# Building one-hot tiles with one two-input instruction for four numbers, in a single-core attention kernel

## The reference

```python
q, k, v = (split_heads(x @ W + b) for W, b in ...)      # 2 batches, 16 heads, 4096 tokens, width 16
scores = einsum('bhqd,bhkd->bhqk', q, k) * scale
sparsity = scores.max(axis=-1) - scores.mean(axis=-1)
_, top_idx = top_k(sparsity, U)                          # U = 307 of 4096 queries for each head
attn = softmax(einsum(q[top_idx], k) * scale)
out = zeros_like(q).at[top_idx].set(attn @ v)
x = layernorm(x + out @ Wo + bo)
x = layernorm(x + rwkv_channel_mix(x))                   # sigmoid(xr Wr) * (relu(xk Wk)^2 Wv)
```

## Time and profile before

| what | value |
|---|---|
| median of the runs | 3358.51 us (3 runs, 3357.48 to 3361.5) |
| profiled execution | 3360.67 us, its span 3358.7 us |
| PE busy | 3050.7 us, 91% of the span |
| DVE busy | 2933.8 us, 87% |
| ACT busy | 2807.1 us, 84% |
| POOL busy | 1573.7 us, 47% |
| mean granted TensorE clock | 0.972 |

### The profile page before, as it was taken

One profiled execution on the slowest core, in us unless ns is written; L12 is line 12 of the kernel. 1 busy time (PEld: TensorE's weight loads), 2 busy tenths in 40 slices (PEclk: granted clock), 3 DMA queues, 4 the chain that ended last, 5 costly groups with the idle time before them and its releaser, 6 DMA issues.

```text
span 3358.7 us, 60170 instructions
## 1 busy us (share of the span) xinstructions
PE 3050.7 (91%) x16612; PEld 1447.7 (43%) x16612; DVE 2933.8 (87%) x5964; ACT 2807.1 (84%) x6118; POOL 1573.7 (47%) x2744
## 2 busy tenths in 40 slices
PE   6999899989989999998998999899998998997587
PEld 3343333444434434443443555444444433444376
DVE  4999999988989888898998999899999898896488
ACT  5999889988988998898898887799987898893455
POOL 3223022224534543653364664766555653556644
PEclk8999999999999999999999999999999999997799
DMA  6342333432241131023112252112251121112122
GB/s 183 83 121 82 85 83 86 78 12 35 39 34 27 33 40 33 15 39 34 33 33 43 48 51 45 35 35 38 41 46 33 38 40 15 33 21 12 18 83 69
DMA packets 263682, 163.72 MB, mean 49 GB/s; under 512 B 168946, under 2 KB 242866, under 8 KB 259250
## 3 DMA queue, kind: packets, MB, share of 16 engines
q1 hardware_dynamic: 255250, 156.41, 25.2%
q0 software_dynamic: 6144, 1.37, 0.5%
q10 hardware_dynamic: 1952, 2.10, 0.2%
HBM read 111.86 MB, written 47.86 MB: 48 GB/s over the span
## 4 chain that ended last, share of the span: by engine, by line
DVE 34%; PE 27%; ACT 21%; issue 14%; POOL 2%; DMA 1%; ACTq 0%; DVEq 0%; SPq 0%; POOLq 0%
DVE JK L1170 27%; ACT AB L1022 18%; PE DP L756 7%; PE CP L737 4%; PE CP L746 4%; ACT E L1057 1%; DVE SPr L1170 1%; PE BP L774 1%; PE PV L864 1%; DVE VF L1382 1%; PE PV L865 1%; DVE fst L1341 1%; PE BP L849 1%; PE PV L887 1%; PE BP L828 1%
## 5 line engine op out<-in xcount | busy, mean ns | idle before, releaser
L1170 DVE CUSTOM_DVE_ANT_0 JK<-DP,AB 128x1024 bf16<-128x1024 f32 x2048 | 2468.1, 1223 | 286.0 <-ACT AB L1022 103.4
L1022 ACT ACTIVATE AB<-CP 128x512 f32<-128x512 f32 x4096 | 2292.8, 623 | 271.9 <-PE CP L737 203.1
L756 PE MATMUL DP<-KS,QS 128*128 128x512 f16 x4096 | 1234.8, 383 | 49.7 <-DVE SPr L1170 41.6
L1603 POOL TENSOR_TENSOR SCR<-E 128x307 f16<-128x307 f32 x966 | 671.7, 707 | 562.0 <-ACT E L1057 555.8
L737 PE MATMUL CP<-KS,QS 128*128 128x512 f16 x2048 | 794.2, 388 | 52.6 <-ACT AB L1022 28.8
L746 PE MATMUL CP<-KS,QS 128*128 128x512 f16 x2048 | 792.9, 387 | 30.3
L756 PEld LDWEIGHTS DP<-KS,QS 128*128 128x128 f16 x4096 | 360.8, 99 | 350.9 <-DVE SPr L1170 145.9
L1057 ACT ACTIVATE E<-BP 128x307 f32<-128x307 f32 x913 | 435.6, 477 | 42.4 <-PE BP L849 37.5
L737 PEld LDWEIGHTS CP<-KS,QS 128*128 128x128 f16 x2048 | 197.7, 97 | 512.8 <-ACT AB L1022 422.0
L746 PEld LDWEIGHTS CP<-KS,QS 128*128 128x128 f16 x2048 | 197.2, 96 | 389.0 <-ACT AB L1022 345.1
L849 PE MATMUL BP<-QT,KA 128*128 128x307 f16 x913 | 270.9, 297 | 28.8 <-ACT QT L1049 19.6
(11 more groups left out here) (386 smaller groups left out, 3138.0 us busy)
## 6 DMA issues: line engine op xcount, KB each, us to landing
KS<-KTC SPq DMA_DIRECT2D x256, 128.0 KB
QS<-QSC SPq DMA_DIRECT2D x512, 64.0 KB
KA<-KTC SPq DMA_DIRECT2D x128, 128.0 KB
QN<-SCR SPq DMA_DIRECT2D x16, 544.0 KB, 3.4
SCR<-in_L_attn_x SPq DMA_DIRECT2D x16, 512.0 KB, 5.5
AO<-E SPq DMA_DIRECT2D x16, 512.0 KB, 7.0
VF<-in_L_attn_x SPq DMA_DIRECT2D x64, 128.0 KB, 2.2
VF<-AO SPq DMA_DIRECT2D x64, 128.0 KB, 2.2
```

The source lines that it names most:

```text
L756: r = pe.matmul(o[:, 512 * j:512 * j + 512], qs, ks[j][:, 0, :], start=True, stop=True)
L1022: act.activation(AB[p % 3][:, 512 * j:512 * j + 512], BANK["C%d" % j], ACT.Abs).then_inc(ab_full, 1)
L1170: dve.tensor_tensor_reduce(out=JK[p % 2][:], in0=BANK["D%d" % u], in1=AB[p % 3][:], scale=1.0, scalar=0.0, op0=ALU.add, op1=ALU.max, accum ...
L1603: pool.tensor_tensor(EL[a % NE], E[a % NE][:], EH[a % NE], ALU.subtract).then_inc(el_g, 1)
```

## The change

The 36 one-input comparisons of a group, each against a constant, become nine two-input comparisons. Each takes the same `fb` or `fa` four times over and compares it with four numbers from a new tile `numbers` (0 to 19, made once by POOL), each read again for all 160 or 96 columns. In the groups selected during the score steps, `ob` and `oa` used to be handed out two planes a step, over 8 + 10 steps; now four a step, over 4 + 5. In the tail it was four a step before too. A semaphore is raised by four at once, so POOL's four multiplications are released together. And `prelude(0)` waits for the end of `values(1)` before it clears its buffers, where before it cleared first.

```diff
         yield [("slots", g)]
...
-        m = 2 if gaps else 4
+        m = 4
         for j in range(0, 16, m):
             yield [("ob", g, j, m)]
         for j in range(0, A_COLS, m):
...
+        while state["arranged"] < HEAD0[g] or "v1" not in done:
+            yield []
         yield [("ka", 0), ("qgzero",)] if g == 0 else []
-        while state["arranged"] < HEAD0[g]:
-            yield []
...
+        numbers = sb("numbers", [128, A_COLS], F16)
...
+            def one_hot(o, v, j0, m, w):
+                return dve.tensor_tensor(o[:, j0:j0 + m, 0:w], v[:, 0:w].unsqueeze(1).broadcast_to([128, m, w]),
+                                         numbers[:, j0:j0 + m].unsqueeze(2).broadcast_to([128, m, w]), ALU.is_equal)
+
             def ob(g, j0, m):
...
-                for j in range(j0, j0 + m):
-                    dve.tensor_scalar(OB[:, j, 0:NT * n], fb[:, 0:NT * n], float(j), None, ALU.is_equal).then_inc(sel_ob, 1)
+                one_hot(OB, fb, j0, m, NT * n).then_inc(sel_ob, m)
 
             def oa(g, j0, m):
-                n = GROUPS[g][2]
-                for j in range(j0, j0 + m):
-                    dve.tensor_scalar(OA[:, j, 0:NT * n], fa[:, 0:NT * n], float(j), None, ALU.is_equal).then_inc(sel_oa, 1)
+                one_hot(OA, fa, j0, m, NT * GROUPS[g][2]).then_inc(sel_oa, m)
...
+                pool.iota(numbers[:], pattern=[[1, A_COLS]], base=0, channel_multiplier=0,
                           allow_small_or_imprecise_dtypes=True)
```

More of the change, by code:

```diff
@@ L1448, in setup @@
                 pool.iota(tokc[:], pattern=[[128, NT]], base=-L // 2, channel_multiplier=1,
+                          allow_small_or_imprecise_dtypes=True)
+                pool.iota(numbers[:], pattern=[[1, A_COLS]], base=0, channel_multiplier=0,
                           allow_small_or_imprecise_dtypes=True)
```

## The result

The changed kernel takes 3365.36 us (median of 20 runs, 3359.01 to 3369.65), the kernel before 3357.80 (20 runs, 3348.31 to 3363.91): a ratio of 1.0022, with a 95% interval of 1.0015 to 1.0029. That is 7.6 us slower; forecast was 17. The profiled execution took 3367.77 us, its span is 3365.8, 7.1 more than before. Of these 7.1, the first `JK` starts 4.0 later, the seven heads with comparisons take 9.2 more, the other heads 2.3 less, and the stretch behind the last `JK` 3.9 less. The last `JK` starts 11.0 us later than before, where 15 to 25 were forecast.

The account below looks back on a forecast made before the run. DVE bounds `ob` and `oa` steps (1.37 us against PE's 1.30), PE the rest. Seven groups +19.6, moved attention +1.4, tail -4: +17.0 us, forecast 3375.5 us (3368 to 3384, chance 0.45; wider range 3357 to 3392).

Parts of the forecast that it names:

- The price of the instruction: New DVE comparison at the slow rate, 1.04 ns a column: 0.74 us paid for a wide one, 0.47 for a narrow.
- pair-rate rival: New comparison runs at 0.53 ns a column: 3358.5 us, or 3349 with short waits too; chance 0.12.
- the waits: DVE's waits for POOL in comparison steps; group 1: 2.5 us removed in eight `ob` steps, 2.6 added in four rounds.
- My middle value: Group 1, three later `ob` rounds and first `oa` round: DVE waits 0.65 us each for POOL's backlog.
- The rival that DVE slips in at once: Waits of only 0.1 or 0.15 us a round, -9.8 us in all, 3366 us; chance 0.20.
- lost cover: Freed steps shorten only as far as PE allows: +1.4 us in group 1, +0.5 each in groups 4 and 5.
- the case I had named last: Prediction is wrong if `feed(0)`'s chain through POOL stretches by more than a wait beside each `ob` round.
- +4.2 was forecast: Group 1, wide and beside attention: net cost over 18 score steps from its first `ob`, +4.2 us.
- 2.1 us credited: Group 2's earlier wait of 3.4 us behind six POOL subtractions will hardly recur; 2.1 us of it credited.
- +0.7 forecast: Group 2's net cost over its 18 score steps, after the credit for its long wait: +0.7 us.
- Attention earlier and the tail: `prelude` nine steps sooner: +1.4 us in score steps, -4 in the tail, with 0 and -7 as its ends.

Follow-up runs that it names:

- The pair read: Changed kernel with every number stored twice and both inputs read as pairs of neighbours, same nine instructions and order: 3350.41 us, 0.9962 of the kernel before.
- The kernel with 252 at the new pace: Changed kernel with the earlier one-input comparisons, 36 a group, four planes a step, no tile numbers: 3372.50 us, 1.0029 of the kernel before.
- that with 18 two-number instructions a group: Two-input comparison with two numbers in one instruction, in the 18 steps and order of the kernel before: 3375.08 us, 1.0029 of it.
- the kernel with steps given back: Changed kernel with nine empty steps after `oa`, so attention starts when it did before: 3374.40 us, 1.0031 of the kernel before.
- the shifted kernel: Changed kernel with group 2's one-hots 14 steps later, behind the indirect DMAs of head 14: 3363.01 us, 0.9996 of the kernel before.
- both profiles: The changed kernel's first profile and that of its unaltered second run, which took 3369.20 us, 1.0017 of the kernel before.

## Why the prediction was half right

**The price of the instruction: right.** 0.817 and 0.549 us measured, 0.82 and 0.554 forecast, and an undisturbed round costs 1.88 and 1.61 us from maximum to maximum, 0.74 and 0.47 above 1.14. The pair read isolates the cause: with the numbers in pairs the same columns take 0.482 and 0.348 us, which is 0.52 ns for each column more, against 1.05. The Trainium skill ("Vector Engine (DVE) Microarchitecture Reference", section 5.1) has one element read 16 times as an input of a two-source operation on 2-byte operands run at one element a cycle, and a row read again and again at two; these runs agree in the factor of two, with 160 and 96 repeats. The pair-rate rival was wrong for the kernel as changed. As a mechanism its price was good: it gave 3358.5 us with the long waits and 3349 with the short ones, and the kernel with pairs had short waits (7.3 us with the tail's) and a ratio that makes 3345 us of 3357.8.

**The step that failed: the waits.** "I take 0.65 in the three later `ob` rounds and the first `oa` round", and "in eight `ob` steps the wait of 0.31". In the seven groups these terms came to 12.8 us of waits removed and 13.2 added, as good as nothing. Measured: 25.6 before, 9.4 after, so 16.2 us less.

Two things were wrong. Nearly half of the waits of before stood beside `oa`, where I had put none: in group 1 2.37 us there and 2.21 beside `ob`. And the new instruction doesn't come back into a backlog. It gets in behind the POOL instruction under way, and POOL pays. So a wait is had per exposed instruction, and there are 63 of them now, not 252. The kernel with 252 at the new pace had 31.7 us of waits, that with 18 two-number instructions a group 20.1, the changed one 9.4. My middle value lay between 0.31 and 1.25, and 0.2 was under both, though I had named "nothing" as a least too. The rival that DVE slips in at once, at 0.1 to 0.15 a round and 3366 us, had the mechanism right here. That its time was only 0.6 off is luck: its waits came to 9.4 us less and not 16.2, and what it lacked there is about what it lacked in the losses below.

**Part of it came back elsewhere.** With 13.5 us for the instructions and -16.1 for the waits the kernel with steps given back should gain 2.6 in its seven heads, and it loses 9.2. The rest is 11.8, where 5.7 of lost cover were forecast. In that kernel PE idles 9.9 us behind POOL in 30 steps each of heads 22 and 27, where before it did not; that is the case I had named last, "if `feed(0)`'s chain through POOL stretches". Whole heads blur this, since their clock differs between executions (head 22 has 4.4 of the 9.9 and lost 0.2). The 18 steps from the first `ob`, which the forecast was made for, are clearer. There the kernel with steps given back loses 10.6 us, and what the instructions and the waits don't explain is 3.6 and 5.9 us in groups 4 and 5, beside 4.4 and 5.5 of this idle time, and 3.7 in the other five groups together, where 4.7 of lost cover were forecast. In group 1 the 18 steps take 29.9 us against 29.8, where +4.2 was forecast.

What makes POOL late for PE is shown in part. The same pace and order with one-input comparisons have none of this idle time, and neither has the changed kernel once the multiplications are moved away from `ob`. So it takes both, the multiplications beside `ob` and the merged instruction. That the instruction does it only by holding POOL up is not shown: with pairs it is shorter, and the idle time is 11.2 us and not 9.7.

**Group 2: the reading of the earlier trace rows failed.** I took it that a backlog may shut DVE out, and that it would hardly happen again (2.1 us credited). It happened again and longer, 5.1 us, so head 14 gained nothing (0.0 and -0.4; +0.7 forecast, which is near by luck, since its other waits went). A backlog alone was not the cause, as the shifted kernel shows: there POOL is as busy, and DVE gets in. What stood ahead of the backlog was.

**Attention earlier and the tail: the sum about right, the parts not.** Forecast were +1.4 and -4. The stretch behind the last `JK` is 317.9 us against 321.8, so -3.9. But from the last instruction of `slots` to the first product pass 10.8 us (10.5 forecast, 13.5 before), which is -2.7; the part ahead of it is 5.1 us longer and not 1 shorter, and what follows `idx` 6.3 shorter. In the score steps heads 28 and 29 take 5.7 us less than before, also in the one-input kernel at the new pace, and 0.6 less with the steps given back: moved attention is a gain there and no loss. By the runs, giving the steps back costs 3 to 5 us (1.0031 against 1.0022 and 1.0017), with intervals that overlap. The first `JK`'s 4.0 us, in no part of the forecast, belong to that execution; the median of 20 runs, 7.6 us above before, doesn't rest on them.

## What to carry to other kernels

Look at how an input is read before you merge small instructions into a large one: a single 16-bit number repeated halved the rate of DVE's comparison here, and storing it twice gave the rate back (here from 1.0022 to 0.9962, and to 0.9921 with eight numbers in one). Where two engines share a lock, count the instructions that are exposed to it, and see from both sides who waits: the time DVE did not lose here was lost by POOL, and what counted was whether somebody waited for POOL. Keep DVE's lock-taking work away from the stretch right behind POOL's indirect DMAs (5.7 us of waits against 0.6 here).

## What the runs showed that I had not expected

**DVE shut out behind indirect DMAs.** In the traces of before, of the changed kernel (both profiles) and of the pair read, I looked at each DVE instruction other than a maximum that took over 2.2 us. Four are two-input operations into `S` near 482 us and one stands at 22 us; each of the other nine lies in a POOL burst that began within 0.04 us of the end of an indirect DMA. Bursts as long without one let DVE in. Counted over all 14 traces, for comparisons that came into a burst of 2.5 us or more with at least 1.5 us of it left: of 529 in bursts without an indirect DMA right ahead none waited over 0.57 us; of 18 that were DVE's first in a burst behind one, 13 waited 1.7 to 6.2 us, and of nine that came later in such a burst none over 0.52. Five of the 18 did get in within 0.54 us, so the DMA is not enough by itself. The smallest, an instruction of 72x2 numbers in the tail of the changed kernel, DVE and then POOL:

```profile
3060.46 3.72 DVE L1233 SCALAR_TENSOR_TENSOR test<-met,ahead_of 72x2 f32<-72x2 f32 x1
```

```profile
3059.09 1.08 POOL L1620 DMA_INDIRECT AO<-OG,idxs  x1 [0.30 <-ACT E L1058]
3060.19 4.62 POOL L1607 TENSOR_TENSOR SCR<-E 128x307 f16<-128x307 f32 x7
```

The Trainium skill ("SBUF — State Buffer", section "SBUF: two separate sides") has it that whichever starts first, a DVE instruction with two inputs in SBUF or a GpSimd one that reads SBUF, gets the shared pair of ports for the whole instruction. The 0.2 us of group 1 agree with that; the 5.67 us of group 2 are several instructions of POOL's, and more than that rule gives. Why an indirect DMA makes this difference no run here shows.

**A stall was mostly paid twice.** After PE had stood 2.64 us behind POOL in head 27, the clock granted in the next 1.90 us was 0.52, nearly all of it at the lower of the two levels (1.2 GHz of 2.4), and 1.00 again from 2600.4 on. After the next stall, of 2.74 us, it was 0.50 from 2604.2 to 2607.0. In 30 steps of head 22 it was 0.94 before and 0.88 after. So part of what a late product costs is in the products behind it. But the link is loose. In this profile, of the 11 stalls of 2 us or more between the first and the last score steps nine had the low clock within 1.5 us of their end, and the clock also fell where PE had not stood at all for long: at 1084.9, in the window of 15.22 us above, its longest idle time in the steps ahead of it was 0.65 us.
